# Three source one-hots on GpSimd, and twelve instead of nine tiles counted before the first transposes

## The chip, the cores and the metric

One Trainium2 chip, one of its cores. The time is the device time of one execution in microseconds (us). The kernel before takes 277.73 us, the median of three runs (277.69 to 277.73).

## What is computed

x is 256 nodes by 512 features. There are 4352 edges given as `src` and `dst`. Four blocks follow each other, each on the layer-normalised x and added to x: a graph diffusion, a mixture of experts, a message passing over edges and a second expert layer. Only the first concerns this case:

```python
h = x @ W + b                       # x is the normalised input
adj = zeros((N, N)); adj[row, col] = 1; adj[col, row] = 1
adj = adj + eye(N)
adj = adj / maximum(adj.sum(axis=1, keepdims=True), 1.0)
out = w[0] * h; cur = h
for i in range(3):
    cur = adj @ cur
    out = out + w[i + 1] * cur
return relu(out)
```

## The kernel before

The 4352 edges are T = 34 tiles of 128, one edge for each partition. TensorE builds the adjacency by counting (`count`, line 1150). For tile t it multiplies a one-hot of the sources (`src_oh[:, t, :]`, 128 edges by 256 nodes, bf16) with a row of steps of the destinations (`steps[:, t, :]`, 258 wide), once for each half of the nodes: two matmuls for a tile, all 34 tiles summed in two PSUM banks. Neighbouring columns of the sum are compared afterwards, which gives the links.

Who makes what: the source one-hots come from VectorE (`one_hots`, line 746), one `tensor_scalar` for a tile, which compares a row of node numbers (`iota_b`, bf16) with the tile's index. The steps come from VectorE where t % 3 == 2 (`by_vector`) and from ScalarE otherwise (`make_steps`, line 516). GpSimd writes constants in the front (zeros, node numbers, identities, lines 423 to 435), and then waits for the normalised x at line 438.

Each engine runs its own list in order, and semaphores order the engines. VectorE's list in the front: convert the indices (lines 761 to 763), source one-hots and vector steps of tiles 0 to 6 (`one_hots(0, OH_A)`, OH_A = 7), wait for x, statistics of both halves (`variance`), tiles 7 and 8 (`one_hots(OH_A, OH_B)`, OH_B = 9), normalise both halves (`normalise`), tiles 9 to 33. ScalarE's list: steps of its first eight tiles (0, 1, 3, 4, 6, 7, 9, 10), two roots of the variances, two copies of broadcast sources, four more steps, two copies of the transposed x (`copy_xnT`), the remaining eleven steps. TensorE's list: warm-up matmuls (line 1113), broadcasts of the sources (line 1146), `count(0, OH_B)`, the transposes of the normalised x (`transpose_xn(0)`, lines 1115 to 1128), `count(OH_B, 18)`, the first part of the projection x @ W (`project`, line 1173), `count(18, T)`, more of the projection while VectorE compares the counts. SyncE's queue issues the loads, first the indices and x.

Of the kernel before, what the change touches and what calls it, by code (L numbers as in the profile page):

```python
# [5 lines left out]
def graph_and_experts(nc, x, src, dst, edge, gnn_w, gnn_b, diff_w, wr, br, wgate, bgate,  # L6
                      w1, w3, w2, coef, paths, ctrl, f1, f2, out):
    F32, BF16, I32 = mybir.dt.float32, mybir.dt.bfloat16, mybir.dt.int32
    ALU, ACT, AX = mybir.AluOpType, mybir.ActivationFunctionType, mybir.AxisListType
# [48 lines left out]
    SPLIT = 8  # L58
    KEPT_AT = BLOCKS[2] - KEPT[2] - (BLOCKS[2] - SPLIT)
    SPLIT_ROWS = 2  # L60
    OH_A, OH_B = 7, 9
    STEP_W = N + 2
    assert sum(BLOCKS) == T and STEPS == 3

    with ExitStack() as ctx:
        def sb(name, shape, dt=F32):
            return ctx.enter_context(nc.sbuf_tensor(name, shape, dt))

        def sem(name):
            return ctx.enter_context(nc.semaphore(name))  # L70
# [48 lines left out]
        iota_b = iota_w[:, 0:N]  # L119
# [9 lines left out]
        idx_f = sb("idx_f", [P, 3, T])  # L129
# [30 lines left out]
        src_oh = take([T, N], BF16)  # L160
# [121 lines left out]

        scatter_tile = {n: t for b in range(NB) for n, t in scatter_order(b)}
        split_tiles = [t for _, t in scatter_order(NB - 1)][BLOCKS[NB - 1] - SPLIT:]

        def gather_bank(t):
# [29 lines left out]
        const = sem("const")  # L316
# [2 lines left out]
        xn_ready, xn_act, centred = sem("xn_ready"), sem("xn_act"), sem("centred")  # L319
        xnT_ps, xnT_a, xnT_v = sem("xnT_ps"), sem("xnT_a"), sem("xnT_v")  # L320

        idx_ready, onehot = sem("idx_ready"), sem("onehot")
        steps_v, steps_a, dst_hot = sem("steps_v"), sem("steps_a"), sem("dst_hot")
        shift_v, shift_a = sem("shift_v"), sem("shift_a")
        h_ps, h_ready = sem("h_ps"), sem("h_ready")
# [34 lines left out]
        def by_vector(t):  # L360

            return t % 3 == 2

        def halves(ap):
            return ap.rearrange("(h p) f -> p h f", p=P)
# [51 lines left out]
        @block.gpsimd  # L417
        def _(pool):
            def eye_of(ap, base, made_at):
                pool.wait_ge(made, made_at)  # L420
                return nc.gpsimd.affine_select(out=ap, in_=ap, compare_op=ALU.not_equal, fill=1.0, base=base,
                                               pattern=[[-1, ap.shape[-1]]], channel_multiplier=1)
            nc.gpsimd.memset(ident[:], 0.0).then_inc(made, 1)
            nc.gpsimd.memset(ident_b, 0.0).then_inc(made, 1)
            nc.gpsimd.memset(eye, 0.0).then_inc(made, 1)
            nc.gpsimd.memset(zero_b[:], 0.0).then_inc(const, 1)
            nc.gpsimd.iota(iota_w[:], pattern=[[1, STEP_W]], base=0, channel_multiplier=0,
                           allow_small_or_imprecise_dtypes=True).then_inc(const, 1)
            nc.gpsimd.iota(node_id[:], pattern=[[P, H]], base=0, channel_multiplier=1,
                           allow_small_or_imprecise_dtypes=True).then_inc(const, 1)  # L430
            nc.gpsimd.memset(eps[:], 1e-5).then_inc(const, 1)
            eye_of(ident[:], 0, 1).then_inc(const, 1)
            eye_of(ident_b, 0, 2).then_inc(const, 1)
            for h in range(H):
                eye_of(eye[:, h, :], P * h, 3).then_inc(const, 1)


            pool.wait_ge(xn_act, 1)
            pool.wait_ge(xn_ready, H + 1)
            nc.gpsimd.memset(spread, 0.0).then_inc(made, 1)  # L440
            for j in range(ROWQ):
                pool.wait_ge(made, 4 + j)
                nc.gpsimd.affine_select(out=spread, in_=spread, compare_op=ALU.not_equal, fill=1.0, base=-j * (RQ + EQX),
                                        pattern=[[-1, EQX], [0, HC * P // EX]], channel_multiplier=1)\
                    .then_inc(sel_ready if j == ROWQ - 1 else made, 1)


            def gather_rows(b):

                if b == 0:  # L450
                    pool.wait_ge(xn_out, 16 * H)
                if b == 2:
                    pool.wait_ge(mults, NP * (b - 1))
                for i in range(0 if b else PE_TILES, BLOCKS[b]):

                    if b == 1 and i >= 4:
                        pool.wait_ge(mults, 4 * (i - 3))
                    if b == 2 and i >= 2:
                        pool.wait_ge(mults, NP + 3 * (i - 1))
                    nc.gpsimd.indirect_dma_start(  # L460
                        out=x1g[b % 2][:, i, :], out_offset=None, in_=xn_rows,
                        in_offset=bass.IndirectOffsetOnAxis(ap=idx_i[:, 0, FIRST[b] + i:FIRST[b] + i + 1], axis=0))\
                        .then_inc(row_in[b], 16)

            pool.wait_ge(cnt_ps, 1)
            nc.gpsimd.memset(rest_sums[0], 0.0).then_inc(cleared[0], 1)

            nc.gpsimd.memset(rest_sums[1][:, 4:, :], 0.0).then_inc(cleared[1], 1)


            pool.wait_ge(hid, HC // 2)
            nc.gpsimd.memset(select, 0.0).then_inc(made, 1)
            nc.gpsimd.iota(tie[:].rearrange("p (g t) -> p g t", t=TG), pattern=[[0, PH], [1, TG]], base=0,
                           channel_multiplier=0, allow_small_or_imprecise_dtypes=True).then_inc(sel_ready, 1)
            se_v = select.rearrange("k (c g e) -> k c g e", g=PH, e=EQ)
            for h in range(H):
                pool.wait_ge(made, 8 + h)
                nc.gpsimd.affine_select(out=se_v, in_=se_v, compare_op=ALU.not_equal, fill=1.0, base=-ES * h,
                                        pattern=[[-EQ, FC], [0, PH], [-1, EQ]], channel_multiplier=1)\
                    .then_inc(sel_ready if h else made, 1)  # L480

            gather_rows(0)
            gather_rows(1)
            gather_rows(2)

        @block.scalar
        def _(act):
# [24 lines left out]

            nc.scalar.activation(root[:, H:H + 1], eps[:], ACT.Sqrt)
            scalar_tiles = [t for t in range(T) if not by_vector(t)]

            def make_steps(lo, hi):
# [192 lines left out]
        def _(dve):  # L709
# [35 lines left out]

            def one_hots(lo, hi):
                for t in range(lo, hi):
                    nc.vector.tensor_scalar(src_oh[:, t, :], iota_b, idx_f[:, 0, t:t + 1], None, ALU.is_equal)\
                        .then_inc(onehot, 1)
                    if by_vector(t):  # L750
                        nc.vector.tensor_scalar(steps[:, t, :], iota_w[:], idx_f[:, 2, t:t + 1], None, ALU.is_le)\
                            .then_inc(steps_v, 1)
# [11 lines left out]
            dve.wait_ge(idx_ready, 3)  # L764
            dve.wait_ge(const, 3)
            one_hots(0, OH_A)
            dve.wait_ge(x_in, 16)
            for h in range(H):
                variance(h)
            one_hots(OH_A, OH_B)  # L770
            for h in range(H):
                normalise(h)
            one_hots(OH_B, T)

            dve.wait_ge(cnt_ps, 1)
# [331 lines left out]
        def _(pe):  # L1107
# [42 lines left out]
            def count(lo, hi):  # L1150

                for t in range(lo, hi):
                    pe.wait_ge(onehot, t + 1)
                    if by_vector(t):
                        pe.wait_ge(steps_v, sum(by_vector(i) for i in range(t + 1)))
                    else:
                        pe.wait_ge(steps_a, sum(not by_vector(i) for i in range(t + 1)))
                    for h in range(H):
                        last = mm(bank[4 + h][:, 0:STEP_W], src_oh[:, t, h * P:(h + 1) * P], steps[:, t, :],  # L1159
                                  start=t == 0, stop=t == T - 1)  # L1160
                if hi == T:
                    last.then_inc(cnt_ps, 1)

            for q in range(2):
                broadcast(q)
            count(0, OH_B)
            transpose_xn(0)
            for q in range(2, QT):
# [8 lines left out]
            def square(to, left, right, done, ready):  # L1177
# [6 lines left out]
                last.then_inc(done, 1)  # L1184

            count(OH_B, 18)
            wait_xnT(0, 0, 0)
            pe.wait_ge(w_in, 16)
            project(0, 0, 1)
            count(18, T)  # L1190
            project(0, 1, 3)
            pe.wait_ge(link_ready, H)
# [276 lines left out]
```

## Time and profile before

| what | value |
|---|---|
| median of three runs | 277.73 us |
| time of the profiled execution | 277.7 us |
| its span, first to last instruction | 275.9 us |
| TensorE matmuls busy | 265.6 us, 96% |
| VectorE busy | 224.9 us, 82% |
| ScalarE busy | 165.8 us, 60% |
| GpSimd busy | 63.1 us, 23% |

The busy time of an engine is an average over stages with different limits; the chain of waits tells which engine sets the end at a given time. Times in the rows are microseconds from the start of the span, where they are not marked ns. A matmul's recorded length contains the time until its result is there, so the pace of a series is read from start to start.

### The profile page before, as it was taken

Reading aid. Unit: us, or ns where it says so; the run is one execution under the profiler, and the core shown is the slowest. Engines: PE = TensorE matmul, PEld = TensorE weight load, DVE = VectorE, ACT = ScalarE, POOL = GpSimd, SP = SyncE. Lnnn points to the kernel's source line nnn. Section 1 sums busy time; section 2 is a strip of 40 time slices with the busy share of each in tenths; the row PEclk is TensorE's granted clock in tenths of the full one; section 3 lists DMA queues with packets and bytes.
Section 4 is the critical chain, followed back from the end, with each engine's and each line's share of the span. In section 5 each row is a group of like instructions: output and inputs, shape, how many; then the busy total and the mean of one; then the engine's idle time right before and its main releaser. Section 6 shows DMA issues by size and latency. Waiting matters only on the chain.

```text
span 275.9 us, 5689 instructions
## 1 busy us (share of the span) xinstructions
PE 265.6 (96%) x1651; PEld 186.7 (68%) x1660; DVE 224.9 (82%) x662; ACT 165.8 (60%) x336; POOL 63.1 (23%) x52
## 2 busy tenths in 40 slices
PE   6999999999999899999999999989999999999996
PEld 4666698886444799997778786756666664468633
DVE  5977565199657999999999999999999987855372
ACT  6920451011526999945788788499988819552260
POOL 4000060060006644304669991000000000000000
PEclk9999999999999999999999999999999999999999
DMA  5799990000014657733250002013544429000002
GB/s 186 242 412 410 442 406 17 0 2 1 1 38 128 179 137 254 223 119 86 66 131 26 2 1 76 4 24 150 159 151 148 154 86 349 27 0 2 2 0 76
DMA packets 12592, 33.91 MB, mean 123 GB/s; under 512 B 3345, under 2 KB 3602, under 8 KB 12306
## 3 DMA queue, kind: packets, MB, share of 16 engines
q1 hardware_dynamic: 10482, 26.73, 26.9%
q0 software_dynamic: 2080, 6.82, 8.6%
q8 instruction: 14, 0.23, 0.4%
q14 instruction: 16, 0.13, 0.2%
HBM read 32.50 MB, written 1.05 MB: 122 GB/s over the span
## 4 chain that ended last, share of the span: by engine, by line
PE 80%; DVE 9%; ACT 6%; issue 3%; DVEq 1%; DMA 1%; ACTq 0%; SPq 0%
PE psum L1326 15%; PE psum L1276 12%; PE psum L1230 10%; PE psum L1329 8%; PE psum L1254 5%; PE psum L1259 4%; PE psum L1402 3%; PE psum L1428 3%; PE psum L1173 3%; DVE big L1021 2%; PE psum L1159 2%; PE psum L1282 2%; PE psum L1317 2%; PE psum L1182 1%; PE psum L1440 1%
## 5 line engine op out<-in xcount | busy, mean ns | idle before, releaser
L460 POOL DMA_INDIRECT big<-xn_rows,big x26 | 51.3, 1974 | 54.5 <-DMA xn_rows<-xn 23.4
L595 ACT ACTIVATE prod<-edges,coef_b 128x320 f32 (+1 forms) x77 | 43.0, 593 | 10.1 <-PE psum L1329 8.4
L1276 PE MATMUL psum<-big,dst_oh 128*128 128x512 f32 x104 | 48.8, 593 | 0.0
L1011 DVE TENSOR_TENSOR prod<-big,prod 128x320 f32<-128x320 f32 (+1 forms) x77 | 40.5, 527 | 0.4 <-DVE big L982 0.2
L1326 PE MATMUL psum<-prod,ident 128*128 128x128 f32 x160 | 32.0, 294 | 0.6 <-DVE prod L1011 0.5
L1326 PEld LDWEIGHTS psum<-prod,ident 128*128 128x128 f32 x160 | 24.4, 190 | 10.0 <-issue 9.1
L1230 PE MATMUL psum<-edges,big 128*128 128x256 f32 x128 | 28.3, 380 | 0.0
L1276 PEld LDWEIGHTS psum<-big,dst_oh 128*128 128x128 f32 x104 | 18.0, 191 | 13.5 <-issue 13.4
L1230 PEld LDWEIGHTS psum<-edges,big 128*128 128x128 f32 x128 | 24.1, 190 | 3.5 <-issue 0.3
L1021 DVE TENSOR_TENSOR big<-big,prod 128x64 f32 (+2 forms) x80 | 26.3, 328 | 0.1
L595 ACT ACTIVATE xparts<-edges,coef_b 128x320 f32 (+1 forms) x45 | 24.2, 584 | 1.1 <-PE psum L1326 0.9
L1011 DVE TENSOR_TENSOR xparts<-big,xparts 128x320 f32<-128x320 f32 (+1 forms) x45 | 23.5, 523 | 0.3 <-ACT xn L595 0.3
L1329 PE MATMUL psum<-prod,ident 128*128 128x64 f32 (+1 forms) x110 | 19.8, 262 | 0.0
L1326 PE MATMUL psum<-xparts,ident 128*128 128x128 f32 x96 | 19.1, 294 | 0.7 <-DVE xparts L1011 0.7
L595 ACT ACTIVATE xn<-edges,coef_b 128x320 f32 (+1 forms) x32 | 17.6, 589 | 0.4 <-PE psum L1326 0.2
L551 ACT ACTIVATE edges<-psum 128x256 f32<-128x256 f32 x8 | 3.1, 384 | 24.2 <-PE psum L1230 18.6
L1011 DVE TENSOR_TENSOR xn<-big,xn 128x320 f32<-128x320 f32 (+1 forms) x32 | 16.8, 525 | 0.3 <-issue 0.2
L1329 PEld LDWEIGHTS psum<-prod,ident 128*128 128x128 f32 x110 | 16.7, 192 | 0.0
L595 ACT ACTIVATE src_t<-edges,coef_b 128x320 f32 (+1 forms) x30 | 16.3, 581 | 0.6 <-PE psum L1326 0.6
L1326 PEld LDWEIGHTS psum<-xparts,ident 128*128 128x128 f32 x96 | 14.1, 190 | 2.9 <-issue 2.6
L1021 DVE TENSOR_TENSOR big<-big,xparts 128x192 f32 (+2 forms) x48 | 15.9, 331 | 0.2 <-issue 0.2
L1011 DVE TENSOR_TENSOR src_t<-big,src_t 128x320 f32<-128x320 f32 (+1 forms) x30 | 15.6, 519 | 0.0
(217 smaller groups left out, 501.1 us busy)
## 6 DMA issues: line engine op xcount, KB each, us to landing
big<-in_w SPq DMA_DIRECT2D x3, 2048.0 KB, 16.2
edges<-in_f SPq DMA_DIRECT2D x11, 512.0 KB, 3.5
edges<-in_edge SPq DMA_DIRECT2D x1, 3584.0 KB, 23.9
edges<-in_edge SPq DMA_DIRECT2D x1, 2560.0 KB, 23.7
edges<-in_edge SPq DMA_DIRECT2D x5, 512.0 KB, 4.2
edges<-in_f SPq DMA_DIRECT2D x1, 2560.0 KB, 10.2
big<-in_gnn_w SPq DMA_DIRECT2D x1, 1024.0 KB, 6.3
xs<-in_x SPq DMA_DIRECT2D x1, 512.0 KB, 3.8
```

Source lines behind the costliest of these rows:

```text
L460: nc.gpsimd.indirect_dma_start(out=x1g[b % 2][:, i, :], out_offset=None, in_=xn_rows, in_offset=bass.IndirectOffsetOnAxis(ap=idx_i[:, 0, F ...
L595: nc.scalar.activation(slot(n)[:, 0:BLOCKS[b], :], segment(edges[:, FIRST[b]:FIRST[b] + BLOCKS[b], :], single_column(words, p)), ACT.Copy, ...
L1011: nc.vector.tensor_tensor(v, segment(xg[:, 0:tiles, :], first_column(words[b], p)), v, ALU.mult).then_inc(mults, 1)
L1021: nc.vector.tensor_tensor(v, v, slot(n)[:, KEPT[b]:BLOCKS[b], :], ALU.add).then_inc(sums, 1)
L1173: last = mm(bank[2 + h], xnT[:, kc, h * P:(h + 1) * P], w_sb[:, kc, :], start=kc == 0, stop=kc == KC - 1)
L1230: last = mm(bank[2 + c % 4][:, n * N:(n + 1) * N], w[:, kc, c * P:(c + 1) * P], xnT[:, kc, :], start=kc == 0, stop=kc == KC - 1)
L1254: last = mm(bank[2 + h], hT[:, c, h * P:(h + 1) * P], w2_sb[:, c, :], start=c == 0, stop=c == HC - 1)
L1259: last = mm(gather_bank(t), src_t[:, h, t * P:(t + 1) * P], xparts[:, k, h, :], start=h == 0 and k == 0, stop=h == H - 1 and k == 2)
L1276: last = mm(bank[2 + h], dst_oh[:, n % DR, h * P:(h + 1) * P], tile_sums(b, t), start=False, stop=False)
L1326: last = mm(path_sums(to), ident[:], product[:, 0:PT].rearrange("p t u -> p (t u)"), start=False, stop=False, skip_group_check=True)
L1329: last = mm(more_sums(b, to), ident[:], product[:, PT:KEPT[b]].rearrange("p t u -> p (t u)"), start=False, stop=False, skip_group_check=True)
L1402: last = mm(bank[2 + k][64 * j:64 * j + 64, i * P:(i + 1) * P], yT[:, kc, c, :], f1_sb[:, kc, c * P:(c + 1) * P], start=k > 0 and kc == 0, ...
```

## The change

GpSimd makes the source one-hots of tiles 9, 10 and 11 (`by_pool`), after its constants, in a list of its own with the semaphore `onehot_pool`; VectorE leaves those three out, but still makes the steps of tile 11. OH_B becomes 12: VectorE handles its part of tiles 7 to 11 in front of the normalisation, and TensorE counts tiles 0 to 11 in front of the transposes and 12 to 17 behind them. ScalarE's list is unchanged.

```diff
-    OH_A, OH_B = 7, 9
+    OH_A, OH_B = 7, 12
+    POOL_LO = 9
...
+        def by_pool(t):
+
+            return POOL_LO <= t < OH_B
...
+            pool.wait_ge(idx_ready, 3)
+            pool.wait_ge(const, 2)
+            for t in range(POOL_LO, OH_B):
+                nc.gpsimd.tensor_scalar(src_oh[:, t, :], iota_b, idx_f[:, 0, t:t + 1], None, ALU.is_equal).then_inc(onehot_pool, 1)
...
             def one_hots(lo, hi):
                 for t in range(lo, hi):
-                    nc.vector.tensor_scalar(src_oh[:, t, :], iota_b, idx_f[:, 0, t:t + 1], None, ALU.is_equal)\
-                        .then_inc(onehot, 1)
+                    if not by_pool(t):
+                        nc.vector.tensor_scalar(src_oh[:, t, :], iota_b, idx_f[:, 0, t:t + 1], None, ALU.is_equal)\
+                            .then_inc(onehot, 1)
...
                 for t in range(lo, hi):
-                    pe.wait_ge(onehot, t + 1)
+                    if by_pool(t):
+                        pe.wait_ge(onehot_pool, t - POOL_LO + 1)
+                    else:
+                        pe.wait_ge(onehot, sum(not by_pool(i) for i in range(t + 1)))
```

## Rows read from the trace of the kernel before

**Rows 1.** The page: the chain that ended last, by engine, shares of the span.
```profile
PE 80%; DVE 9%; ACT 6%; issue 3%; DVEq 1%; DMA 1%; ACTq 0%; SPq 0%
```

**Rows 2.** The chain in order of time, first 20 us: start us, us, what.
```profile
3.74 0.68 DVE big L748 x3
...
7.02 0.18 DVE mv L721
...
7.88 0.56 DVE xn L728
...
9.79 2.17 PE psum L1159 x18
...
12.83 3.54 PE psum L1159 x32
```

**Rows 3.** TensorE's timeline (start us, us, operation, count, idle before); last, line 1159.
```profile
4.48 3.82 PE L1159 MATMUL psum<-big 128*128 128x258 bf16 x18
8.48 1.31 PE L1126 MATMUL psum<-ident,xn 128*128 128x128 f32 x8 [0.18 <-DVE xn L728]
9.63 0.38 PE L1159 MATMUL psum<-big 128*128 128x258 bf16 x2
...
3.67 1.01 PE L1146 MATMUL psum<-edges 128*128 128x128 bf16 x8
5.55 1.06 PE L1159 MATMUL psum<-big 128*128 128x258 bf16 x4
7.06 1.24 PE L1159 MATMUL psum<-big 128*128 128x258 bf16 x6
11.80 1.03 PE L1173 MATMUL psum<-big,edges 128*128 128x512 f32 x2
16.21 0.59 PE L1173 MATMUL psum<-big,edges 128*128 128x512 f32 x1
...
L1159 PE MATMUL psum<-big x18: 270/422/422, 4.5 to 8.0; 128*128 128x258 bf16 x18
```

**Rows 4.** Timeline of ScalarE: the roots, and the last two steps.
```profile
6.96 0.57 ACT L490 ACTIVATE root<-mv,eps 128x1 f32<-128x1 f32 x2
14.56 0.90 ACT L519 ACTIVATE big<-iota_w,idx_f 128x258 bf16<-128x258 bf16 x2
```

**Rows 5.** Timelines of VectorE and of the DMA queue around x, and x's landing.
```profile
5.52 0.68 DVE L720 BATCH_NORM_STATS2 stats<-xs 128x6 f32<-128x512 f32 x1
...
1.65 0.44 SPq L376 DMA_DIRECT2D xs<-in_x  x1
...
xs<-in_x SPq DMA_DIRECT2D x1, 512.0 KB, 3.8
```

**Rows 6.** GpSimd: timeline of the front's end, and its selects by form.
```profile
2.47 1.01 POOL L421 TENSOR_SCALAR_AFFINE_SELECT edges<-edges 128x128 bf16<-128x128 bf16 x3
34.08 0.31 POOL L440 MEMSET edges<- 128x256 f32 x1 [30.60 <-DVE xn L728]
...
L443 POOL TENSOR_SCALAR_AFFINE_SELECT edges<-edges 128x256 f32<-128x256 f32 x4 | 1.7, 415 | 0.6
```

**Rows 7.** VectorE's one-hots of the destinations beside GpSimd, and after it: timelines.
```profile
57.06 0.28 POOL L473 IOTA tie<- 128x128 f32 x1
57.30 3.64 POOL L478 TENSOR_SCALAR_AFFINE_SELECT select<-select 128x512 bf16<-128x512 bf16 x2
...
57.03 4.24 DVE L757 TENSOR_SCALAR big<-iota_w,idx_f 128x256 bf16<-128x256 bf16 x8
57.42 1.71 DVE L757 TENSOR_SCALAR big<-iota_w,idx_f 128x256 bf16<-128x256 bf16 x1
61.52 1.84 DVE L757 TENSOR_SCALAR big<-iota_w,idx_f 128x256 bf16<-128x256 bf16 x9
...
L478 POOL TENSOR_SCALAR_AFFINE_SELECT select<-select x2: 1734/1747/1760, 57.3 to 59.2; 128x512 bf16<-128x512 bf16 x2
```

**Rows 8.** Windows: busy of PE, PEld, DVE, ACT, POOL (count), then clock, DMA.
```profile
5.00:10.00 5.00, 4.76 (x29) 3.06 (x28) 4.86 (x21) 5.00 (x15) 0.00 (x0) 1.00 0.72 253
```

More of the change, by code:

```diff
@@ L320, in graph_and_experts @@
         xnT_ps, xnT_a, xnT_v = sem("xnT_ps"), sem("xnT_a"), sem("xnT_v")
-        idx_ready, onehot = sem("idx_ready"), sem("onehot")
+        idx_ready, onehot, onehot_pool = sem("idx_ready"), sem("onehot"), sem("onehot_pool")
         steps_v, steps_a, dst_hot = sem("steps_v"), sem("steps_a"), sem("dst_hot")
```

## The prediction

> **What bounds the kernel now.** I start with the chain of waits that ended last, by engine [rows 1]: 80% of the span is TensorE, so an engine that runs beside TensorE matters only where TensorE waits for it. Then the same chain in order of time for the first 20 us [rows 2]. From 3.74 to 8.43 us it is VectorE, without a gap: the seven first source one-hots and their two step tiles, the statistics of both halves of x (the second ends at 7.20), one-hots 7 and 8, steps 8, and the normalisation of the first half. From 8.48 us [rows 3] it is TensorE: eight transposes, the 18 matmuls of tiles 9 to 17, half a projection chunk (two instructions), 32 matmuls of tiles 18 to 33. So two things count in the front: whatever lengthens VectorE before 8.43 us delays the whole kernel one for one, and whatever TensorE no longer has to do after 8.48 us is won. Third, the timelines of TensorE, ScalarE and VectorE around that point [rows 3 to 5]. TensorE counts nine tiles between 4.48 and 8.30 us, waits 0.18 us for the normalised half, and starts its next count at 9.63 us. ScalarE has no idle time from its roots at 6.96 us to 15.46 us. x itself was issued at 1.65 us and takes 3.8 us to land, 5.45 us, and the statistics start at 5.52 us [rows 5]: VectorE has no wait there that could take up a delay.
>
> The program's span is 275.9 us and that execution took 277.7 us, so 1.8 us lie around the span; its time is the median of the runs (277.73) within 0.03 us. A change of the span is therefore added to 277.73.
>
> **Part 1, three tiles counted earlier (removed from behind the transposes, added in front).** A pair of matmuls of one tile takes 3.54 / 16 = 0.221 us at the pace of [rows 2]. In front, tile 8's second matmul, the last of 18, starts at 4.48 + 3.82 - 0.27 = 8.03 us [rows 3], so TensorE is free for tile 9 at 8.14 us and for the transposes at 8.14 + 3 x 0.221 = 8.80 us, instead of 8.48: 0.32 us late. The transposes take 9.63 - 8.48 = 1.15 us; behind them stand six tiles, not nine: 9.95 + 6 x 0.221 = 11.28 us, against 11.80 now [rows 3] (the 2.17 us of now hold 0.18 us of waits for VectorE's step tiles, which go, since VectorE is then ahead). That is 0.52 us early at the projection.
>
> **Part 2, VectorE's order.** Source one-hots 9, 10 and 11 go (nine instructions take 5.52 - 3.74 = 1.78 us, 0.20 each [rows 2, 5]), but steps of tile 11, a vector tile, now stands in front of the normalisation: +0.20 us. The normalised half comes at 8.63 us and can be used at about 8.68, under the 8.80 of part 1, so it costs nothing; if TensorE were not busy there it would cost those 0.20 us. The 0.60 us taken off VectorE lie off the path: the chain is on TensorE from 8.48 us to the end of the count [rows 2, 3].
>
> **Part 3, what is late next.** ScalarE's steps for tiles 9 and 10 are among its first eight, done before 6.96 us. The last two, of tiles 31 and 33, end at 14.56 + 0.50 = 15.06 and at 15.46 us [rows 4]. TensorE would start tile 31 at 12.14 + 13 x 0.221 = 15.02 and must wait to about 15.11 (0.05 us of handover, as 8.43 to 8.48 in [rows 2, 3]); tile 33 then ends at 15.77 us, where the next projection instruction now starts at 16.21. So 0.08 of the 0.52 us is lost to ScalarE: **0.44 us gained, before GpSimd's price.** What follows is TensorE, ScalarE and VectorE in turn on data of this count, nothing there is timed by the clock on the wall, so it moves along.
>
> **Part 4, what GpSimd's three one-hots cost VectorE.** GpSimd's last instruction of the front ends at 3.48 us and the next is at 34 us [rows 6], so its own time is free, and it has the tiles long before 8.1 us. It waits for the converted indices, as VectorE does, so it starts at about 3.8 us, exactly beside VectorE's one-hots of 3.74 to 5.52 us, the chain. The trace shows once what that means. From 57.03 us VectorE runs the same form of instruction (128x256, bf16 to bf16, compare with an index): eight take 4.24 us while GpSimd runs two selects of 1.75 us each; nine without GpSimd take 1.84 us [rows 7]. At 0.197 us each, eight should take 1.65, so 2.59 us were lost to 3.49 us of GpSimd: 0.74 us per us. GpSimd's select works on a tile in SBUF and holds VectorE out for most of its length. No row shows a GpSimd compare with an index. Nearest is its select over 128x256 at 0.41 us [rows 6]: 3 x 0.41 x 0.74 = 0.92 us. The low bound is 0: GpSimd's iota at 57.06 us, written beside the first two one-hots, left their steps at 0.20 us (two from 57.03 to 57.42 [rows 7]), and only short parts of an instruction may collide. The high bound is the costly select's rate: 1.75 / 512 x 256 = 0.87 us each, 3 x 0.87 x 0.74 = 1.94 us. I take 0.92, because size and engine are those of the 0.41 us row.
>
> A delay X of VectorE in that stretch passes whole into everything behind: the statistics, the roots on ScalarE (two from 6.96 to 7.53 us, the second 0.29 long and so from 7.24 us, 0.04 after its variance [rows 2, 4]), so ScalarE's copies and steps, the normalisation and the transposes. TensorE's first seven tiles hide it (it takes 0.21 us a matmul there and reaches tile 6 at 7.06 us, VectorE is through with it at 5.5 [rows 3, 5]), but tile 7 waits. So the end moves by X - 0.44: with 0.92 it is +0.48 us, **278.2 us**; with 0 it is 277.3; with 1.94 it is 279.2.
>
> Two statements of the Trainium skill bear on it. The Trainium skill's page "SBUF — State Buffer", section "Who interferes with whom", says that a `tensor_scalar` of VectorE in a two-port mode and any GpSimd instruction share a port pair by an exclusive lock, whoever issues second standing still for the whole of the other. The trace agrees in kind, but shows 74% and not the whole; by the rule the price would be 3 x 0.41 = 1.23 us and the time 278.5. The Trainium skill's page "GPSIMD Engine Reference", section 3.1, gives about 1.8 cycles per element at 1.2 GHz for a good loop, an estimate of 0.38 us for 256 elements; three of these alone would be 1.15 us and the time 278.4. Both fall to rival (a) below, at its near edge.
>
> **The clock.** The granted clock is given as 1.00 from 5 to 10 us [rows 8], but the matmuls' own pace tells more: until 7.06 us they step by (1.06 - 0.42) / 3 = 0.21 us [rows 3], the 1.2 GHz level, and the counts behind the transposes step by 0.11, the 2.4 GHz level. The last matmuls in front of them are recorded with 0.27 instead of 0.42 us [rows 3], so the rise was before 8.0 us. Before the rise TensorE was busy without a gap from 3.67 us [rows 3]. The three tiles moved come after the rise, at 0.221 each.
>
> **Rivals.** (a) GpSimd's instructions run at the costly rate, 0.6 to 0.9 us each or more, and VectorE stands still for 1.1 to 2 us: 278.4 to 279.2 us, so beyond 0.2% of slowing. For it: [rows 7], where GpSimd took 3.4 ns per element; against it: the 0.41 us of [rows 6]. It decides when X passes 1.0 us. (b) No collision, since the parts that need the memory are short: X under 0.3, 277.3 to 277.6 us. Against it: the 2.59 us of [rows 7]. This is the only way to a gain, and even whole it is 0.16%. (c) The clock rises later, because TensorE now has holes while VectorE stands: 8 transposes and 12 matmuls at the lower level are 1.15 + 1.33 = 2.5 us more, 280.7 us. Against it: TensorE's first seven tiles are not starved until X passes some 1.3 us.
>
> **How the numbers follow.** Chances: forecast (X 0.3 to 1.0) 0.47, (a) 0.38, (b) 0.11, (c) 0.04. A measurement of this kernel can tell about 0.2%, 0.55 us, from no change. Slower by more needs X above 1.0: (a) and (c), 0.42. Faster by more is out of reach by the sum (0.44 at best), 0.03 for a term that I have too large. The rest, 0.55, is within. Range: from the floor of the sum, 277.3, to the high bound of the unknown price, 279.2; outside are (c) and the far ends of (a) and of the handovers in part 3.
>
> **What would show it.** Right: VectorE's one-hots 0 to 6 with some steps far above 0.20 us; the first statistics at 6.4 us instead of 5.52; the first transposes at 9.7; first projection instruction 11.28 + X; first instruction behind the count at 15.77 + X. GpSimd's three in the stretch 3.8 to 5.5. Wrong: statistics still at 5.5 us (b), or the pace of 0.21 us after 7.5 us (c), or a shift at 16.2 us that is no longer there at the end of the span.

## The result

The changed kernel takes 282.07 us (median of four runs, 281.91 to 282.18), the kernel before 277.73; the ratio is 1.0156, 95% interval 1.0143 to 1.0168. The forecast was 278.2 us with 277.3 to 279.2 as range. The profiled execution has a span of 280.4 us.

The front shows what was forecast, smaller. VectorE's timeline of the kernel after: the first three one-hots, which take 0.90 us instead of the 0.68 of [rows 2], the steps behind them, and the statistics; below them the second and the third one-hot by themselves, 0.42 us from start to start where the others step by 0.20.

```profile
3.75 0.90 DVE L759 TENSOR_SCALAR big<-iota_w,idx_f 128x256 bf16<-128x256 bf16 x3
4.58 0.41 DVE L762 TENSOR_SCALAR big<-iota_w,idx_f 128x258 bf16<-128x258 bf16 x1
5.97 0.68 DVE L730 BATCH_NORM_STATS2 stats<-xs 128x6 f32<-128x512 f32 x1
...
3.96 0.50 DVE L759 TENSOR_SCALAR big<-iota_w,idx_f 128x256 bf16<-128x256 bf16 x1
4.38 0.27 DVE L759 TENSOR_SCALAR big<-iota_w,idx_f 128x256 bf16<-128x256 bf16 x1
```

GpSimd's three comparisons beside them, and TensorE's transposes, the counts behind them, the first projection and the first instruction behind the last count (after; [rows 3] has those of before):

```profile
3.82 3.02 POOL L446 TENSOR_SCALAR big<-iota_w,idx_f 128x256 bf16<-128x256 bf16 x3 [0.32 <-DVE idx_f L774]
...
9.26 1.18 PE L1137 MATMUL psum<-ident,xn 128*128 128x128 f32 x8
10.28 1.55 PE L1173 MATMUL psum<-big 128*128 128x258 bf16 x12
11.67 0.59 PE L1187 MATMUL psum<-big,edges 128*128 128x512 f32 x1
16.33 0.59 PE L1187 MATMUL psum<-big,edges 128*128 128x512 f32 x1
```

The first instruction behind the last count starts at 16.33 us in the kernel after, 0.12 us late (16.21 before). So the front explains 0.12 of 4.3 us. The page tells where to look: the chain that ended last, by engine, which for the kernel before is [rows 1] and had no GpSimd in it.

```profile
PE 64%; POOL 14%; DVE 10%; ACT 5%; issue 3%; DMA 2%; DVEq 1%; ACTq 1%; SPq 0%; POOLq 0%
```

14% of 280.4 us is one instruction. The chain in order of time, kernel after, 140 to 190 us:

```profile
144.89 38.34 POOL big L470
183.23 0.30 POOLq L66
183.54 3.67 DMA big<-xn_rows,big
```

That is line 460 of the kernel before: GpSimd's indirect DMA of `gather_rows`, which fetches the normalised rows of one tile of edges for the message passing. Block 2 (tiles 24 to 33, ten gathers) is fetched while VectorE still multiplies block 1. Most of these instructions take about 1 us, the fifth about 5 (4.91 before, 5.24 after). The ninth takes 20.58 us in the kernel before and 38.34 after. GpSimd's timeline, first the kernel before (fifth, ninth and tenth), then after (ninth and tenth):

```profile
134.19 4.91 POOL L460 DMA_INDIRECT big<-xn_rows,big  x1 [1.79 <-DVE prod L1011]
...
144.81 20.58 POOL L460 DMA_INDIRECT big<-xn_rows,big  x1 [1.19 <-DVE prod L1011]
165.69 1.03 POOL L460 DMA_INDIRECT big<-xn_rows,big  x1 [0.30 <-DVE prod L1011]
```

```profile
144.89 38.34 POOL L470 DMA_INDIRECT big<-xn_rows,big  x1 [1.19 <-DVE prod L1022]
183.54 0.94 POOL L470 DMA_INDIRECT big<-xn_rows,big  x1 [0.30 <-issue]
```

Before, the last rows were there at about 169 us and block 2 began at 182.4, so the 20.58 us cost nothing. After, VectorE stands still for 4.99 us at the start of block 2 (its timeline, kernel after):

```profile
182.00 0.41 DVE L1032 TENSOR_TENSOR big<-big,prod 128x256 f32 x1
187.39 0.49 DVE L1022 TENSOR_TENSOR xparts<-big,xparts 128x320 f32<-128x320 f32 x1 [4.99 <-DMA big<-xn_rows,big]
```

So the question is why a gather 130 us behind the change takes 18 us longer. The instructions of VectorE beside it are the same in both, a multiplication (128x448) and an addition (128x256) in turn, each with two inputs in SBUF, 0.87 us a pair. There is one difference: near the end of the 20.58 us VectorE makes a short pause in the kernel before, and none in the kernel after. VectorE's timelines near 164.6 us, before, then after:

```profile
163.96 0.61 DVE L1011 TENSOR_TENSOR src_t<-big,src_t 128x448 f32<-128x448 f32 x1
164.60 0.43 DVE L1021 TENSOR_TENSOR big<-big,src_t 128x256 f32 x1
```

```profile
164.04 0.61 DVE L1022 TENSOR_TENSOR src_t<-big,src_t 128x448 f32<-128x448 f32 x1
164.57 0.41 DVE L1032 TENSOR_TENSOR big<-big,src_t 128x256 f32 x1
```

It is 0.64 us from start to start in the kernel before against 0.53 after. In both kernels an instruction load (queue q14 of the DMA view) starts between 165 and 166 us.

### The profile page after: what moved, and what is told of

Read it like the earlier page. It is cut to its first block, busy times and chain, and to the rows that moved or that the text cites. A ratio compares the mean times of both kernels' runs of the same rounds, so it can differ in the third digit from the quotient of the medians.

```text
span 280.4 us, 5690 instructions
## 1 busy us (share of the span) xinstructions
PE 267.8 (96%) x1651; PEld 187.3 (67%) x1660; DVE 225.0 (80%) x659; ACT 164.8 (59%) x336; POOL 83.6 (30%) x55
## 4 chain that ended last, share of the span: by engine, by line
PE 64%; POOL 14%; DVE 10%; ACT 5%; issue 3%; DMA 2%; DVEq 1%; ACTq 1%; SPq 0%; POOLq 0%
POOL big L470 14%; PE psum L1340 10%; PE psum L1244 10%; PE psum L1343 6%; PE psum L1290 6%; PE psum L1268 5%; PE psum L1273 4%; PE psum L1416 3%; PE psum L1442 3%; DVE big L1032 2%; PE psum L1187 2%; PE psum L1173 2%; PE psum L1296 2%; DMA big<-xn_rows,big 1%; PE psum L1196 1%
## 5 line engine op out<-in xcount | busy, mean ns | idle before, releaser
L470 POOL DMA_INDIRECT big<-xn_rows,big x26 | 68.9, 2648 | 54.6 <-DMA xn_rows<-xn 23.5
L1340 PE MATMUL psum<-xparts,ident 128*128 128x128 f32 x96 | 20.0, 299 | 2.5 <-DVE xparts L1022 2.5
```

Source lines behind the costliest of these rows:

```text
L470: nc.gpsimd.indirect_dma_start(out=x1g[b % 2][:, i, :], out_offset=None, in_=xn_rows, in_offset=bass.IndirectOffsetOnAxis(ap=idx_i[:, 0, F ...
L1340: last = mm(path_sums(to), ident[:], product[:, 0:PT].rearrange("p t u -> p (t u)"), start=False, stop=False, skip_group_check=True)
```

## The experiments

Three theories went in. Theory 1: the gather is held as long as VectorE's two-input instructions follow each other without a pause; a pause falls where VectorE's list crosses into newly loaded instructions, so it moves with the length of that list, and the change took three instructions out of it. Theory 2: the front's shift of 0.1 us changes how gather and multiplications meet. Theory 3: GpSimd is slower after its comparisons. All ratios below are to runs of the kernel before on the same chip.

**e1: the kernel after, three tiny instructions back in VectorE's list.**

```diff
             one_hots(OH_B, T)
+            for i in range(3):
+                nc.vector.memset(spare[:, i:i + 1], 0.0)
```

> The kernel after, with three tiny VectorE writes (one column each, into a spare tile) behind its last source one-hot, where VectorE waits for the count anyway (about 15.5 to 16.4 us). VectorE's list is as long as before again from there on. Theory 1 (place in the list): the gather that took 38.3 us after the change is let in by a short pause of VectorE, and where that pause falls goes by VectorE's position in its list; with three instructions back it falls near 164.6 us again, the gather takes about 20.6 us and the time is 277.8 to 277.9. Theory 2 (timing): the 0.1 us shift out of the front changed how gather and multiplications meet; it is still there, so the gather takes 38 us and the time is about 282. Theory 3 (GpSimd itself is in another state after its three comparisons): also about 282.

277.84 us, ratio 1.0006 (0.9997 to 1.0016). The 4.3 us are gone but for some 0.1 us, though three instructions were added. GpSimd's and VectorE's timelines of e1:

```profile
144.93 20.58 POOL L471 DMA_INDIRECT big<-xn_rows,big  x1 [1.19 <-DVE prod L1025]
...
164.07 0.62 DVE L1025 TENSOR_TENSOR src_t<-big,src_t 128x448 f32<-128x448 f32 x1
164.73 0.42 DVE L1035 TENSOR_TENSOR big<-big,src_t 128x256 f32 x1
```

The pause is back (0.66 us from start to start), the gather takes 20.58 us to the hundredth, and GpSimd's comparisons and the front's shift of 0.11 us are still there. Theories 2 and 3 are out for this kernel.

**e2: the kernel before, three instructions less.** Of the sixteen constant writes in VectorE's routing stage five are done in two, as runs of equal values: 13 in all, with the same values.

```diff
+            nc.vector.memset(low[:, 3, 0:3], 1.0)
+            nc.vector.memset(low[:, 2, 0:2], 1.0)
             for i in range(G):
                 for j in range(G):
-                    last = nc.vector.memset(low[:, i, j:j + 1], 1.0 if j < i else 0.0)
+                    if not (i >= 2 and j < i):
+                        last = nc.vector.memset(low[:, i, j:j + 1], 1.0 if j < i else 0.0)
```

> The kernel before, with 13 instead of 16 of the tiny constant writes of VectorE in the routing (runs of equal values written at once, same values; near 38 us, beside TensorE's expert matmuls). The front is untouched and GpSimd makes no one-hot. Theory 1: VectorE's list is three shorter from there on, as after the change, so the gather of block 2 takes about 38 us and the time is about 282. Theories 2 and 3: 277.7, the gather 20.6 us.

282.00 us, ratio 1.0155 (1.0138 to 1.0172). Nothing of the change is in this kernel, and it is as slow. GpSimd's timeline of e2:

```profile
144.71 38.34 POOL L460 DMA_INDIRECT big<-xn_rows,big  x1 [1.20 <-DVE prod L1014]
183.35 0.95 POOL L460 DMA_INDIRECT big<-xn_rows,big  x1 [0.31 <-issue]
```

With e1 this shows the cause of the loss from both sides: the length of VectorE's list in front of the gather.

**e3: the new order alone, without GpSimd.** OH_B = 12 in the kernel before.

> The kernel before with OH_B = 12 alone: VectorE makes the source one-hots 9 to 11 itself, in front of the normalisation. VectorE's list has the same length. Working of the prediction: four more instructions of 0.20 us in front of the normalised half, three of them not in the kernel after, so the first transposes come at about 9.2 us, and the first instruction behind the count about 0.2 to 0.3 us later than before (16.4 to 16.5 us). Theory 1: the gather stays at about 20 us, time 277.9 to 278.0. Theory 2: the shift of the front alone can flip it, time about 282. Theory 3: 277.9 to 278.0, as theory 1.

277.71 us, ratio 1.0000 (0.9991 to 1.0010), the gather at 20.58 us. The first instruction behind the count starts at 16.21 us, exactly as before, though the transposes are late by 0.8 us (9.27 against 8.48 in the chain): what they lose, the six matmuls fewer behind them and the waits for VectorE's steps give back. My 0.2 to 0.3 us were too many.

**e4: the kernel after, with one break in VectorE's stream.**

```diff
                     multiply(n + 1)
+                if n == NP + 22:
+                    nc.vector.memset(spare[:, 0:1], 0.0)
                 add(n)
```

> The kernel after with one tiny VectorE write between a multiplication and an addition of block 1 (behind multiplication 23 of that block), about 2 us after the long gather starts. If the gather is held by VectorE's two-input instructions following each other without a pause, it is let in there: its length falls from 38 us to 2 to 4 us, the wait of 5.0 us before block 2's first multiplication goes, and the time is 277.8 to 278.0. If it is held by something else (a slow memory, its own queue, another engine), it stays at 38 us and the time at about 282.

277.69 us, ratio 0.9997 (0.9987 to 1.0006). GpSimd's and VectorE's timelines of e4:

```profile
145.05 3.16 POOL L471 DMA_INDIRECT big<-xn_rows,big  x1 [1.19 <-DVE prod L1023]
...
147.32 0.42 DVE L1033 TENSOR_TENSOR big<-big,xn 128x256 f32 x1
147.34 0.06 DVE L1040 MEMSET spare<- 128x1 f32 x1
147.66 0.61 DVE L1023 TENSOR_TENSOR prod<-big,prod 128x448 f32<-128x448 f32 x1
```

An instruction that costs VectorE next to nothing ends the hold 0.87 us later. So it is VectorE's uninterrupted stream that holds the gather, not a slow memory or GpSimd's own queue. That the two meet at a shared memory path is how I read it; no run here looks at the path itself.

**e5: GpSimd's comparisons moved beside VectorE's statistics**, on top of e4.

```diff
             pool.wait_ge(const, 2)
+            pool.wait_ge(onehot, OH_A)
             for t in range(POOL_LO, OH_B):
```

> The kernel of e4 (after, with the tiny VectorE write in block 1), in which GpSimd waits until VectorE has made source one-hots 0 to 6 and so compares beside VectorE's statistics. In the kernel after each of GpSimd's three comparisons cost VectorE 0.15 us (0.45 us in all), beside one-hots. If it is the memory path of VectorE's one-hots that collides, the first statistics come at 5.5 us again and the comparisons run freely beside them; the loss that is left is from one-hots 7 and 8 and the two step tiles, at most 0.3 us, the first instruction behind the count starts at 15.9 to 16.2 us and the time is 277.3 to 277.7. Rival: GpSimd costs VectorE its 0.15 us each wherever it stands; then 16.3 us and 277.7 as in e4.

277.26 us, ratio 0.9986 (0.9977 to 0.9995). VectorE's timeline of e5, then TensorE's first instruction behind the count:

```profile
5.52 0.69 DVE L732 BATCH_NORM_STATS2 stats<-xs 128x6 f32<-128x512 f32 x1
...
7.50 0.72 DVE L764 TENSOR_SCALAR big<-iota_w,idx_f 128x258 bf16<-128x258 bf16 x2
8.14 0.15 DVE L739 RECIPROCAL rstd<-root 128x1 f32<-128x1 f32 x1
...
15.95 0.59 PE L1191 MATMUL psum<-big,edges 128*128 128x512 f32 x1
```

The statistics are back at 5.52 us with GpSimd running beside them, so these don't collide; the one-hots and step tiles do. What is left is a delay of 0.22 us there, from the third comparison, which starts at 7.65 us. In the kernel after it's the first two comparisons that collide, for 0.23 and 0.22 us; the third starts at 5.89 us, stands beside the statistics and costs nothing. So the price is 0.22 to 0.23 us for a comparison beside one-hots or step tiles, not 0.15 us for each of three, as the expectation has it. The time is just below the expected 277.3 to 277.7. The front is now 0.26 us ahead of the kernel before, where the change as made was 0.12 behind.

**e6: the kernel before, with e4's break.**

> The kernel before with the tiny VectorE write of e4. Theory 1: its gather of 20.6 us falls to about 3 us too; since its rows were in the memory long before block 2 asked for them (165.7 + 3.7 against some 182 us), nothing is gained: 277.6 to 277.8. Rival: the held gather costs something in the kernel before as well; then the time falls below 277.5.

277.39 us, ratio 0.9990 (0.9981 to 0.9999). The gather fell to 3.16 us, as expected, but the time fell too, by 0.25 us, which I had given to the rival. The gather isn't why: see e10.

**e7: the kernel after, gathers of block 2 without their waits.**

```diff
-                    if b == 2 and i >= 2:
-                        pool.wait_ge(mults, NP + 3 * (i - 1))
```

> The kernel after, whose gathers of block 2 no longer wait for VectorE's multiplications one by one: all ten are issued one behind the other from 126 us on. Theory 1: what matters is only that no gather is still held when block 2 begins; with 1.25 us each they would be through at 139 us, and even if one is held until VectorE's pause near 138.7 us, the rest pass right behind it, all by 145 us; time 277.8 to 277.9. Rival: every gather beside VectorE's two-input instructions can be held to the end of block 1; then 38 us or more again, and 282 us or over.

277.30 us, ratio 0.9988 (0.9978 to 0.9997). One gather is held, for 5.85 us, and let in by VectorE's pause near 138.7 us; the others follow, and the last starts at 143.98 us. The time is lower than expected by 0.5 us; e7's list is three instructions shorter than that of the kernel before, and e10 bears on it.

**e8: e1 with one instruction back instead of three.**

> As e1, but one tiny VectorE write instead of three. Theory 1 says that VectorE's position decides: with three back the pause fell in front of an addition and let the gather in at 165 us, with none back it vanished. One back is between the two, so either 277.8 or 282, nothing between them, and the trace shows a pause of some 0.1 us near 165 us in the first case and none in the second. A time of about 280.6, a third of the way, would speak for a cost that grows with the number of instructions and against theory 1.

277.40 us, ratio 0.9991 (0.9982 to 1.0001). The gather takes 20.92 us, so it was let in near 165.6, but VectorE's pause there is almost nothing. VectorE's timeline of e8:

```profile
163.80 0.62 DVE L1024 TENSOR_TENSOR src_t<-big,src_t 128x448 f32<-128x448 f32 x1
164.34 0.42 DVE L1034 TENSOR_TENSOR big<-big,src_t 128x256 f32 x1
164.69 0.63 DVE L1024 TENSOR_TENSOR prod<-big,prod 128x448 f32<-128x448 f32 x1
```

It is 0.35 us from the addition to the next multiplication, where it is 0.33 or 0.34 elsewhere: 10 to 20 ns were enough. The gather is let in at one point or not at all, as theory 1 says, and a cost for each instruction is out. Two things were expected otherwise: a pause of some 0.1 us, and 277.8 us; the time is 0.4 us lower.

**e9: e7 and e5's order of GpSimd together, without any tiny write.** The diffs are those of e5 and e7.

> The kernel of e7 (after, gathers of block 2 without their waits) with GpSimd's comparisons moved behind VectorE's source one-hot 6, as in e5 (no tiny write). e5's front gained 0.26 us at the first instruction behind the count (15.95 against 16.21 us), e7's gather order is through before block 2. If both add up: 276.8 to 277.1. Rival: what e7 and e8 gained over e1 (0.3 to 0.5 us) lies in how VectorE's list falls into its loads, and another list gives it back: 277.2 to 277.4.

276.93 us, ratio 0.9974 (0.9964 to 0.9984): 0.72 us under the kernel before on that chip (277.65), and the fastest of the study, within what was expected. GpSimd's timeline of e9 from its one held gather on:

```profile
133.30 5.85 POOL L469 DMA_INDIRECT big<-xn_rows,big  x1 [0.30 <-issue]
139.46 1.19 POOL L469 DMA_INDIRECT big<-xn_rows,big  x1 [0.30 <-issue]
...
143.60 0.94 POOL L469 DMA_INDIRECT big<-xn_rows,big  x1 [0.30 <-issue]
```

Its first instruction behind the count starts at 15.95 us, as in e5.

**e10: the kernel before without the gathers' waits.**

> The kernel before with the gathers of block 2 without their waits, nothing else. VectorE's list and the front are those of the kernel before. Theory 1: no gather was on the path, so 277.6 to 277.7. Rival: the held gather also slows VectorE or the rest in the kernel before, then 277.3, as in e7.

277.71 us, ratio 1.0002 (0.9993 to 1.0011): the held gather costs the kernel before nothing. So e6's 0.25 us don't come from the gather; what is left is its one added instruction. The traces agree: the pause of 0.11 us near 164.6 us stands in the kernel before, e1, e3 and e10, whose lists are equally long there, and not in e5 to e9; and the same four have another pause at 208 us, which in the kernel before is (VectorE's timeline)

```profile
207.78 0.49 DVE L1011 TENSOR_TENSOR xparts<-big,xparts 128x320 f32<-128x320 f32 x1
208.45 0.36 DVE L1021 TENSOR_TENSOR big<-big,xparts 128x192 f32 x1 [0.18 <-issue]
```

It is 0.67 us from start to start instead of 0.40. In e6 VectorE is 0.10 us ahead of the kernel before from the first of these points on and 0.30 us from the second, and the span ends 0.3 us earlier (275.6 against 275.9). At the end of block 2 the chain of the kernel before is on VectorE's additions, one behind the other until 226 us:

```profile
219.91 0.30 DVE big L1021
```

The traces also say where the pauses stand in the list. I count VectorE's records from the first, those of register instructions included. In all fourteen kernels the point near 165 us is the 704th record. In the kernel before, e1, e3 and e10 that record is an addition, and it is 0.11 to 0.13 us late. In e4, e5 and e8 it is a multiplication, 10 to 20 ns late. In the kernel after, e2, e6, e7, e9, e11 and e12 it is a register instruction that runs while VectorE still multiplies, and the addition behind it is at most 2 ns late. No other multiplication or addition between 150 and 181 us is more than 4 ns late in any of them. The instruction load on q14 starts 0.6 to 0.7 us behind that record each time, also where nothing is let in, so the load by itself doesn't end the hold. That newly loaded instructions begin at these points, as theory 1 has it, is a reading; the runs show the fixed place in the list and the load near it. In the kernel before the late additions at 138.35 and 208.45 us are the 576th and the 960th record, so these points are 128 records apart or a multiple of that. A held gather ends soon behind such a point: by 0.79 us in the kernel before (165.39 against 164.60), 0.78 in e1 and 0.88 in e8, as by 0.87 us behind e4's write; the fifth gather of the kernel before ends 0.75 us behind the 576th record.

**e11: the kernel after with e5's order of GpSimd alone.**

> The kernel after with GpSimd's comparisons moved behind VectorE's source one-hot 6, and nothing else. VectorE's list is that of the kernel after, so by theory 1 there is again no pause near 165 us and the gather is held to the end of block 1: 38 us, and the time is 281.4 to 281.9, the front's 0.26 us being swallowed or kept. Theory 2 (timing of the front decides): the front is now earlier than in the kernel before, so the gather may come free: 277.3.

281.67 us, ratio 1.0144 (1.0129 to 1.0160), gather 38.34 us again, with the front at 15.96 us. The front is earlier here than in the kernel before, and the gather is held all the same: theory 2 is out a second time.

**e12: the kernel after, gathers of block 2 waiting for additions instead of multiplications** (`sums` for `mults` in the two lines of e7).

> The kernel after, whose gathers of block 2 wait for VectorE's additions instead of its multiplications, at the same numbers: each starts about 0.3 us later, against another point of VectorE's pair of instructions. If a gather is held whenever VectorE's two-input instructions follow without a pause, wherever it starts: 38 us again and about 282. If only a start together with a multiplication is unlucky (the two held ones start 0.01 to 0.02 us behind one), none is held for long, and the time is 277.3 to 277.9.

280.69 us, ratio 1.0110 (1.0095 to 1.0125). Another gather is held, the last, for 34.53 us from 148.71 us until VectorE stops, and one of 6.71 us before it. Neither outcome came quite as expected; it is nearer the first. The hold lasts to the same end as after, but no further gather stands behind this one, and the loss is 3.0 us instead of 4.3. The gather starts 0.34 us behind a multiplication, so a start together with one is no condition. Why some gathers pass in 0.95 us beside the same instructions and others are held, no run settles.

## Why the prediction was wrong

**The front's mechanism was right, its sizes were not.** VectorE's statistics started at 5.97 us instead of 5.52, so X was 0.45 us and not 0.92. Part 4 multiplied terms that were off. A GpSimd comparison takes 1.08, 1.02 and 0.95 us here, not 0.41 (the row of its select was no guide to its comparison). VectorE lost 0.23 us to the first and 0.22 to the second, 0.2 us per us of GpSimd and not the 0.74 of [rows 7], and nothing to the third, which ran beside the statistics; the sum had all three beside one-hots. The length was too small, the rate and the number too large. The low end, 0, and the high end, 1.94, did hold X; the two prices worked out beside the sum, 1.23 and 1.15 us, were too high too.

**Parts 1 and 2 held.** With X = 0.45 the working gives transposes at 9.25 us (measured 9.26) and the projection at 11.73 (11.67).

**Part 3, ScalarE's handover, was mis-sized.** As the sum has it, TensorE waits for ScalarE at tile 31. The step of tile 31 ends at 15.52 us (15.06 + 0.46), but its first matmul starts at 15.67: 0.14 us of handover, not 0.05. Timelines of ScalarE and TensorE, kernel after:

```profile
15.02 0.50 ACT L529 ACTIVATE big<-iota_w,idx_f 128x258 bf16<-128x258 bf16 x1
...
15.67 0.82 PE L1173 MATMUL psum<-big 128*128 128x258 bf16 x6
```

Tile 33 doesn't wait. So the count was through, and the next instruction started, at 16.33 us and not at 16.23, 0.12 us late instead of level. e1, which has the front of the kernel after and a list of VectorE as long as before, measured 277.84 against 277.72, the same 0.12 us, though the interval of its ratio also allows for no difference.

**The step that failed** is the sentence at the end of part 3, that nothing behind the count is timed otherwise, "so it moves along". It was argued from the chain of [rows 2], which ends where I stopped reading. Neither the forecast nor a rival had a gather in it. The forecast, slower by 0.5 us, and rivals (a) and (c) have the right sign by luck: the cause they name gave 0.12 us. GpSimd's list shows in the kernel before a gather of 20.58 us among others of mostly 1 us, beside a VectorE that never idles; the 3 x 0.20 us that part 2 "took off VectorE" also took three instructions out of its list, and in this kernel that alone costs 4.3 us (e2). The question to ask was what ends the 20.58 us. It had 13 us of room to the start of block 2, and its end hung on a pause of 0.11 us.

**The clock** rose at the same place: in both kernels the counting matmuls are recorded with 0.42 us up to 7.07 us (the 1.2 GHz level) and with 0.27 to 0.28 us from 7.9 us on (the 2.4 GHz level), under a granted clock of 1.00. Rival (c) didn't occur.

## What to carry to other kernels

Before changing a tuned kernel, look for instructions that take many times the length of their like, also off the chain, and ask what ends them: if it is a chance pause of another engine, any change of that engine's list can put them on the path. Give such a wait a sure end: issue GpSimd's indirect DMAs early enough to be held once and still be in time (e7, e9), or put a break into VectorE's stream where they stand (e4). And before crediting or blaming an edit, pad the list back to its old length (e1) or shorten the old kernel's (e2): here that moved 4.3 us, while the edit's own front was 0.12 us late as made and, with GpSimd beside the statistics, 0.26 us early.

## What the runs showed of the hardware

- GpSimd's indirect DMA can be held by VectorE's `tensor_tensor` with two inputs in SBUF for as long as these follow each other without a pause: 20.58, 34.53 and 38.34 us. Others pass the same stream in 0.95 us. The Trainium skill's page "SBUF — State Buffer", section "Who interferes with whom", tells of a probe in which `tensor_tensor` did not stall such DMAs, and gives a reason that it marks as inferred; the measurement here speaks against it.
- A pause of 10 to 20 ns (e8), or one VectorE write of a single column (e4), lets it in.
- VectorE pauses for 0.01 to 0.27 us at fixed points of its list, seen at records 576, 704 and 960; which instruction falls on the point decides the length, and on a register instruction there was no pause at 704. A list shorter by two instructions made the whole kernel 0.4 us faster (e8 against e1, by their ratios), more than the edit under test.
- A GpSimd comparison of 128x256 bf16 with an index takes 0.92 to 1.08 us, 3.6 to 4.2 ns per element, where VectorE steps by 0.20 us. It costs VectorE's one-hots 0.22 to 0.23 us and its statistics nothing (after, e5).
